# A graph layer on one core: the attention's linear part as columns of the projection's weights, a Gram block moved among the projected chunks, the takes planned anew, the RMS weights loaded as rows

## The reference

```python
xn = layernorm(x)
# attention over the graph (GATv2)
h = (xn * rsqrt(mean(xn**2) + 1e-6) * rms_w) @ W_down          # 1024 -> 256
xl, xr = h @ Wl, h @ Wr                                        # 4 heads of 64
msg = xl[src] + xr[dst]                                        # loops added
e = einsum(where(msg > 0, msg, 0.2 * msg), att)
p = exp(e - segment_max(e, dst)); alpha = p / segment_sum(p, dst)
gnn = segment_sum(alpha * xl[src], dst) @ W_up                 # 256 -> 1024
# linear attention without softmax
q, k, v = xn @ Wq.T + bq, xn @ Wk.T + bk, xn @ Wv.T + bv
mix = ((q @ k.T) * SCALE) @ v @ Wo.T + bo
x = x + gnn + mix
# feed-forward on values rounded to FP4 blocks of 16
g, u = fp4(layernorm(x)) @ fp4(gate_w).T, fp4(layernorm(x)) @ fp4(up_w).T
x = x + fp4(silu(g) * u) @ fp4(down_w).T
```

## Time and profile before

| | us |
|---|---|
| runs: median (lowest to highest), 3 runs | 902.01 (901.41 to 905.28) |
| the profiled execution: its time | 905.27 |
| the profiled execution: span of the instructions | 903.4 |
| TensorE busy | 855.8 (95%) |
| VectorE busy | 794.7 (88%) |
| ScalarE busy | 563.1 (62%) |
| GpSimd busy | 497.2 (55%) |

### The profile page before, as it was taken

How to read it: one execution, slowest core, us unless ns; L and a number is a source line. 1 busy time by engine, 2 the same in 40 slices (tenths; PEclk the granted TensorE clock), 3 DMA queues, 4 the chain that set the end, 5 groups by cost and what they waited for, 6 DMA issues and landing times.

```text
span 903.4 us, 9499 instructions
## 1 busy us (share of the span) xinstructions
PE 855.8 (95%) x2744; PEld 421.2 (47%) x2754; DVE 794.7 (88%) x903; ACT 563.1 (62%) x1977; POOL 497.2 (55%) x527
## 2 busy tenths in 40 slices
PE   6899999999999999999999999999699999999855
PEld 5786455644444444444444444444244444444322
DVE  6999989689999999999999999999993078788994
ACT  3317532387658778779898988789894243243432
POOL 3405588667667677777777878877751130010001
PEclk7989999999999999999999999999699999999878
DMA  9331773735354433554336634338936563222335
GB/s 300 112 124 25 230 200 102 246 89 88 73 177 148 122 88 102 192 186 120 100 99 195 195 97 103 90 92 193 265 84 134 116 155 93 79 43 46 47 47 88
DMA packets 66578, 114.83 MB, mean 127 GB/s; under 512 B 29575, under 2 KB 36516, under 8 KB 66506
## 3 DMA queue, kind: packets, MB, share of 16 engines
q0 software_dynamic: 22144, 63.68, 30.2%
q1 hardware_dynamic: 44378, 50.51, 17.4%
HBM read 89.28 MB, written 17.17 MB: 118 GB/s over the span
## 4 chain that ended last, share of the span: by engine, by line
DVE 59%; PE 32%; issue 4%; ACT 3%; DMA 1%; SPq 0%; ACTq 0%; POOL 0%; DVEq 0%
PE acc L782 21%; DVE acc_sb L1540 11%; DVE z L1703 10%; DVE turned L1532 10%; DVE turned L1701 10%; PE acc L939 2%; PE acc L972 2%; PE turned L939 2%; PE acc L942 2%; PE turned L996 1%; ACT round_mem L1177 1%; DVE z L1708 1%; DVE big_b L1492 1%; DMA big_b<-in_x 1%; DVE big_a L1495 1%
## 5 line engine op out<-in xcount | busy, mean ns | idle before, releaser
L564 POOL DMA_INDIRECT round_mem<-msg_table,idx x352 | 349.5, 993 | 103.0 <-issue 82.6
L1177 ACT ACTIVATE round_mem<-round_mem,pz 128x65 f32<-128x65 f32 x1408 | 354.0, 398 | 6.8 <-DVE acc_sb L1540 2.8
L782 PE MATMUL acc<-wslot,big_a 128*128 128x512 f32 x512 | 220.3, 593 | 0.0
L782 PEld LDWEIGHTS acc<-wslot,big_a 128*128 128x128 f32 x512 | 97.3, 190 | 121.3 <-issue 121.1
L1540 DVE TENSOR_REDUCE acc_sb<-round_mem 128x260 f32<-128x1820 f32 (+1 forms) x62 | 121.6, 1962 | 14.1 <-ACT round_mem L1177 12.0
L782 PE MATMUL acc<-big_b,wslot 128*128 128x512 f32 x256 | 110.0, 593 | 0.0
L782 PE MATMUL acc<-wslot,big_b 128*128 128x512 f32 x256 | 110.0, 593 | 0.0
L1532 DVE TENSOR_TENSOR turned<-round_mem,turned 128x1560 f32<-128x1560 f32 (+1 forms) x62 | 105.4, 1700 | 2.3 <-DMA round_mem<-msg_table,idx 0.2
L1703 DVE TENSOR_REDUCE z<-turned 128x24 f32<-128x1560 f32 (+1 forms) x62 | 105.1, 1696 | 2.1
L1167 ACT ACTIVATE pz<-z 128x7 f32<-128x7 f32 (+1 forms) x248 | 55.4, 295 | 78.9 <-DVE z L1708 77.9
L1701 DVE SCALAR_TENSOR_TENSOR turned<-turned,att_sb 128x1536 f32<-128x1536 f32 (+1 forms) x62 | 103.6, 1671 | 0.1
(11 more groups left out here) (231 smaller groups left out, 1009.8 us busy)
## 6 DMA issues: line engine op xcount, KB each, us to landing
big_b<-in_x SPq DMA_DIRECT2D x12, 512.0 KB, 9.8
round_mem<-msg_table,idx POOLq DMA_INDIRECT x352, 2.8
big_b<-big_b POOLq DMA_DIRECT2D x9, 512.0 KB, 5.9
out_x<-big_b SPq DMA_DIRECT2D x9, 512.0 KB, 3.1
out_x<-acc_sb POOLq DMA_DIRECT2D x9, 512.0 KB, 5.6
wslot<-in_wv_t SPq DMA_DIRECT2D x2, 2048.0 KB, 9.9
wslot<-in_wk_t SPq DMA_DIRECT2D x2, 2048.0 KB, 9.4
wslot<-in_wo_t SPq DMA_DIRECT2D x2, 2048.0 KB, 9.6
```

Source lines behind the costliest of these rows:

```text
L564: pool.indirect_dma_start(xg[g % 4][:, j, :], None, msg_table, bass.IndirectOffsetOnAxis(idx[:, c, j0 + j:j0 + j + 1], 0)).then_inc(xg_in[ ...
L782: mm = nc.tensor.matmul(o(acc[:, n % 4, :]), a, b, start=first, stop=last)
L1177: ins = nc.scalar.activation(to[:, :, j], xg[g % 4][:, j, h * HR + 1:(h + 1) * HR], ACT.Copy, scale=pz[:, g % 2, j, h:h + 1])
```

## The change

- **Linear part.** Wl and Wr are stored head by head as 65 columns (`wlr_sb`, 1 + 64), and VectorE writes -0.2 times the linear weights into the first column of each head. A chunk is two lr groups of 260 columns, one for Wl and one for Wr; the products into `lin_ps` and the 20 small takes go. ScalarE takes 260 columns in one instruction (the last chunk's Wl group in two). Wl and Wr come by four DMAs, in pieces of 256 B.
- **Gram block.** Gram block 0 stands behind the fourth lr group, the order of the first eight blocks is another, and ScalarE ranks six chunks of nodes there in one go before it takes the block.
- **Plan.** The constants of the planning loop change, ScalarE may be given a bank that is full up to 2.5 later than the round's begin, and its banks count as free 3.6 after it. The sums for the bias start a round earlier.
- **RMS weights.** They come as 8 rows of 128, are transposed by TensorE and copied by ScalarE to `rms_col`.
- **Tail.** SiLU waits for the gate half of the product (`gate_full`), VectorE for the whole (`gu_full`); the last chunk's gate and up product stands ahead of the down product of its turn.

```diff
-PRODUCTS_AT, GROUP_STEP = 168, {"p0c": 2.0, "bias": 1.0}
-ROUND_0_AT, SLOT_STEP, ROUND_OVER, TAKE_STEP = 158, 0.95, 2.2, 0.7
+PRODUCTS_AT, GROUP_STEP = 169.5, {"p0c": 2.0, "bias": 1.0}
+ROUND_0_AT, SLOT_STEP, ROUND_OVER, TAKE_STEP = 166.5, 0.95, 2.2, 0.7
...
-BIAS_SUMS_AT, AHEAD = 43, 2
+BIAS_SUMS_AT, AHEAD = 42, 2
...
-GRAM = [(m, 1) for m in (4, 0, 5, 1, 6, 2, 7, 3)] + [(m, 0) for m in (0, 4, 1, 5, 2, 6, 3, 7)]
+GRAM = [(m, 1) for m in (0, 4, 1, 5, 2, 6, 3, 7)] + [(m, 0) for m in (0, 4, 1, 5, 2, 6, 3, 7)]
...
-    g += [("lr", c, "act") for c in range(C)]
-    for kind, eng in (("gram", "act"), ("p", "dve"), ("kv", "dve"), ("t1", "act"), ("t2", "act")):
+    g += [("lr", i, "act") for i in range(4)] + [("gram", 0, "act")] + [("lr", i, "act") for i in range(4, 2 * C)]
+    g += [("gram", i, "act") for i in range(1, 16)]
+    for kind, eng in ( ("p", "dve"), ("kv", "dve"), ("t1", "act"), ("t2", "act")):
...
-        wlr_sb = big_a[:, KB * HID:KB * HID + 4 * HID].rearrange("p (k d) -> p k d", k=2)
-        hid_t = big_a[:, 3072:3072 + 2 * NP].rearrange("p (k n) -> p k n", k=2)
+        wlr_sb = big_a[:, KB * HID:KB * HID + 4 * H * MR].rearrange("p (b h d) -> p b h d", b=4, h=H)
...
-                    with nc.allow_non_contiguous_dma(reason="columns of small vectors"):
-                        sp.dma_start(rms_col[:], rms_w.rearrange("(k p) -> p k", p=P)).then_inc(rms_in, 16)
+                    sp.dma_start(rms_rows[:], rms_w.rearrange("(k p) -> k p", p=P)).then_inc(rms_in, 16)
...
-            sp.dma_start(wlr_sb[:, :, 0:HID], wl.rearrange("(k p) d -> p k d", p=P)).then_inc(wlr_in, 16)
-            sp.dma_start(wlr_sb[:, :, HID:2 * HID], wr.rearrange("(k p) d -> p k d", p=P)).then_inc(wlr_in, 16)
+            for k in range(2):
+                for side, w in enumerate((wl, wr)):
+                    sp.dma_start(wlr_sb[:, 2 * k + side, :, 1:MR],
+                                 w[k * P:(k + 1) * P, :].rearrange("p (h d) -> p h d", h=H)).then_inc(wlr_in, 16)
...
-            sp.wait_ge(lin_taken, 1)
+            sp.wait_ge(lr_taken, 1)
+            sp.wait_ge(acc_taken["act"], taken[index_of["lr", 2 * C - 1]])
...
-            for c in range(2):
-                turn_rows(c)
+            turn_rows(0)
+            pe.wait_ge(rms_in, 16)
+            nc.tensor.transpose(rms_ps, rms_rows[:], ident[0:KB, 0:KB]).then_inc(rms_tp, 1)
+            turn_rows(1)
...
-            for c in range(C):
-                pe.wait_ge(acc_taken["act"], taken[index_of["hid", 2 * (c // 2) + 1]])
-                group("lr", c, [(lambda a: a[0:NC, :], hid_t[:, k, c * NC:(c + 1) * NC], wlr_sb[:, k, :],
-                                 k == 0, k == 1) for k in range(2)])
-                for k in range(2):
-                    mm = nc.tensor.matmul(lin_ps[:, c, :], hid_t[:, k, c * NC:(c + 1) * NC],
-                                          watt[:, 2 * k:2 * k + 2, :].rearrange("p a h -> p (a h)"), start=(k == 0), stop=(k == 1))
-            mm.then_inc(lin_full, 1)
...
+            for i in range(2 * C):
+                c, side = divmod(i, 2)
+                if i == 4:
+                    gram(0)
+                if side == 0:
+                    pe.wait_ge(acc_taken["act"], taken[index_of["hid", 2 * (c // 2) + 1]])
+                group("lr", i, [(lambda a: a[0:NC, 0:H * MR], hid_t[:, k, c * NC:(c + 1) * NC],
+                                 wlr_sb[:, 2 * k + side, :, :].rearrange("p h d -> p (h d)"), k == 0, k == 1) for k in range(2)])
...
-                mm.then_inc(gu_full, 1)
+                    mm.then_inc(gate_full if h == 0 else gu_full, 1)
...
+                if k + 1 == C - 1:
+                    gate_up(k + 1)
                 if 0 <= k - 2 < C:
                     down(k - 2)
-                if 0 <= k + 1 < C:
+                if 0 <= k + 1 < C - 1:
...
-                full = max(at, freed.get(n - 4, 0)) + GROUP_STEP.get(kind, 7.0)
-                if full > begun:
+                full = max(at, freed.get(n - 4, 0)) + GROUP_STEP.get(kind, 6.93)
+                if full > begun + (2.5 if engine == "act" else 0.0):
                     break
                 round_of[n], at = g, full
                 begun += TAKE_STEP if engine == "dve" else 0.0
-                freed[n] = begun + 0.8
+                freed[n] = begun + (0.8 if engine == "dve" else 3.6)
...
+                    both = a[0:NC, 0:H * MR].rearrange("p (h d) -> p h d", d=MR)
+                    to = (acc_sb, xr_sb)[side][:, c, :].rearrange("p (h d) -> p h d", h=H)
+                    scale = rrms[:, c:c + 1]
+                    if side == 0 and c == C - 1:
+                        nc.scalar.activation(to[:, :, 0], both[:, :, 0], ACT.Identity, scale=scale, bias=far_col[:, 0:1]).then_inc(lr_taken, 1)
+                        nc.scalar.activation(to[:, :, 1:MR], both[:, :, 1:MR], ACT.Copy, scale=scale).then_inc(t, 1)
+                    else:
+                        nc.scalar.activation(to[:, :, 0:MR], both, ACT.Copy, scale=scale).then_inc(t, 1)
...
-            act.wait_ge(rms_in, 16)
+            act.wait_ge(rms_tp, 1)
+            nc.scalar.copy(rms_col[:], rms_ps).then_inc(rms_taken, 1)
+            act.wait_ge(rms_taken, 1)
             act.wait_ge(wd_in, 16)
-            for k in range(3):
+            for k in range(2):
...
-            for c in range(3):
-                rank(c)
+            rank(0)
             for c in range(C):
-                take(index_of["lr", c])
-                if c + 3 < C:
-                    rank(c + 3)
-            act.wait_ge(lin_full, 1)
-            for c in range(C):
-                nc.scalar.activation(acc_sb[:, c, 0:ROW:HR], lin_ps[:, c, 0:H], ACT.Identity, scale=rrms[:, c:c + 1],
-                                     bias=far_col[:, 0:1] if c == C - 1 else 0.0)
-                ins = nc.scalar.activation(xr_sb[:, c, 0:H * MR:MR], lin_ps[:, c, H:2 * H], ACT.Copy, scale=rrms[:, c:c + 1])
-            ins.then_inc(lin_taken, 1)
...
-                    act.wait_ge(gu_full, c + 1)
+                    act.wait_ge(gate_full, c + 1)
...
-                                         wlr_sb.rearrange("p k (a h d) -> p (k a) h d", a=2, h=H),
+                                         wlr_sb[:, :, :, 1:MR],
...
-            nc.vector.tensor_scalar(watt[:], watt[:], -SLOPE, None, ALU.mult).then_inc(watt_done, 1)
+            nc.vector.tensor_scalar(wlr_sb[:, :, :, 0], watt[:], -SLOPE, None, ALU.mult).then_inc(watt_done, 1)
...
+                    dve.wait_ge(gu_full, c + 1)
```

More of the change, by code:

```diff
@@ L853, in sum_places @@
                     pe.wait_ge(sort_part, 2)
[L855 removed]
+            for i in range(1, 16):
                 if i == 8:
                     sum_places()
[L858 to L866 removed]
+                gram(i)
             def halves_in(kind, i, first_use):
@@ L1130, in _ @@
             act.wait_ge(key_in, 32)
[L1131 to L1132 removed]
+            rank(0)
             for c in range(C):
[L1134 to L1142 removed]
+                take(index_of["lr", 2 * c])
+                take(index_of["lr", 2 * c + 1])
+                if c == 1:
+                    for i in range(1, 7):
+                        rank(i)
+                    take(index_of["gram", 0])
+                if 7 <= c + 5 < C:
+                    rank(c + 5)
             for i in range(16):
[L1144 removed]
+                if i > 0:
+                    take(index_of["gram", i])
                 if i < KB:
```

42 lines of the change are left out of this document (20 added, 22 removed).

## The result

The changed kernel takes 881.96 us (median of 4 runs, 881.28 to 882.76), the kernel before 903.49 (4 runs, 901.41 to 905.28): a ratio of 0.976, 95% interval 0.974 to 0.979. That is 21.5 us less; forecast were 23.3, and 879. The profiled execution took 882.22 us, span 880.5.

The account below looks back on a forecast made before the run. TensorE and VectorE were both taken as bounds in the long middle. RMS rows 3.8, projection 3.7, replanned takes 12.5 and tail 3.3 sum to 23.3 us off the 902.0 median: 879 forecast, range 870 to 892.

Parts of the forecast that it names:

- The RMS rows: Start of the kernel: loading the RMS weights as rows starts VectorE's third chunk sooner and saves 3.8 us.
- Without rms_col W_down begins ... near 5.3: First loads: without the column load ahead of it, W_down starts near 5.3 us instead of 9.7, 4 us sooner.
- The lower bound of 1.0: Start of the kernel: the RMS weights' gain is only 1.0 us if VectorE's gain does not pass on.
- The projection and the Gram block: Linear part before the attention: four products of 260 columns a chunk and the new order save 3.7 us, bounds 2.5 and 4.4.
- The replanned takes: Long middle: 72 takes moved one to three rounds earlier close TensorE's two waits, saving 12.5 us, bounds 6 and 13.4.
- kv 10: Product n = 27 in the rounds: VectorE's worst wait for a full bank, 3.2 us.
- too tight: Rival, rounds: early takes make them later than 3.3 us and the attention ends last; 886 at 10 us late; chance 0.16.
- Such waits don't add: Rounds: once late, all later slacks are larger, so rounds are late by 3.2 us at most, 2 to 2.5 at the end.
- The slower rival: Rounds: each of 41 earlier ScalarE takes costs beyond the cover; a loss from 27.5 us late on, 0.67 a take; chance 0.03.
- The tail: After the attention: SiLU waiting for the gate half only and the last gate product's order save 3.3 us, bounds 1 and 5.
- one lies off the path: Tail: of VectorE's three waits for ScalarE's normalization, 4.2 us in all, one does not count, leaving 2.0 us.
- sum of the upper bounds: Whole kernel: all four parts at their upper bounds save 26.7 us, giving 875.3 us.

## Why the prediction was right, and where it was not

The sum of 23.3 us came out as 21, with the mechanisms as forecast in three of four parts. In the fourth, the load of the RMS weights, the mechanism was not there. That the time still came within 3 us of 879 is in part luck: 3.8 us were missing there, and the runs found up to 1.8 more in the tail than the sum had.

**The RMS rows: 3.8 forecast, 0.1 measured.** The step that failed is "Without rms_col W_down begins ... near 5.3". It took the order of landings in one trace for a cause: rms_col landed late in it, W_down later, the chunk last. In two other traces with the column the chunk starts at 11.7, as with the rows. Late landings of rms_col and of W_down came together (7.4 and 9.9 us, against 4.7 and 5.0 with 8.2), and which of them makes the other late, or whether both have one cause, no run shows. The slow microsecond is real (76 GB/s in the stretch 5 to 6 of both, 61 in the earlier trace rows, 150 with the rows), but 74 GB/s more for 1 us are 0.07 MB, which is 0.2 us at 418 GB/s, and even that isn't seen. The rule of the Trainium skill (DMA: Bandwidth & Descriptors, "Why a DMA increments its semaphore by 16 and not by 1") says when a DMA counts as landed. I drew from it what a late landing does to the next DMA, which it doesn't say, and the runs don't bear it out: behind the column W_down landed 8.2 us after its issue in two of three traces, behind the rows 7.6 to 8.6 in nine. The lower bound of 1.0 was too high as well. That the projection started at 12.43 instead of 14.52 belongs in the main to the same chance: with the column back it started at 12.38, and in the second trace of before at 13.29. The four loads of Wl and Wr in small pieces, priced at up to 6 us if uncovered, were covered: no engine waits for their landing in the changed kernel's two traces.

**The projection and the Gram block: 3.7 forecast, 3.2 measured** (21.55 - 18.34 in the traces; no run undoes this part whole). A chunk takes 1.755 us, 1.75 were forecast. A small matmul of before thus cost (2.16 - 1.755)/4, some 0.10 us. The Trainium skill (TensorE: Matmul & The Clock Gate, "Back-to-back issue gap") was weighed here with its 25 ns, which it gives as a floor and not as a price; the same section says that in a stream each matmul's weight load counts too. The trace of before agrees: each of the four had a weight load of 128x128, and three of these follow each other in 0.41 us, some 0.11 apart, where one is busy 0.19:

```profile
79.24 0.41 PEld L836 LDWEIGHTS turned<-watt,big_a 128*128 128x128 f32 x3 [0.24 <-issue]
```

TensorE waited some 0.8 us where 1.0 was forecast. That both halves must go together was not in the prediction: the columns alone lose 2.2 us, since ScalarE's 2.31 us a chunk, which I had as the price of a rank and two takes, then is the step.

**The replanned takes: 12.5 forecast, 12.3 measured,** 13.46 between the first traces. The worst wait was forecast at kv 10 with 3.2 us; VectorE stood 1.0 us there and 3.0 in four waits. The rounds end 2.0 us late, 2 to 2.5 were forecast. The forecast that the attention then lands just before TensorE needs it holds. My formula for the case "too tight" (697.5, less what the products start sooner, plus what the rounds are late) can be held to the run with earlier takes: 697.5 - (175.40 - 170.28) + (527.5 - 511.5) = 708.4, and TensorE started its transposes at 708.29 (511.5 is 686.92, the last close of the trace before, less 175.40). What does not hold is "Such waits don't add". Held against the run with takes a round later, where VectorE never waits for a product (510.6 us), the changed kernel's rounds are late by 2.9 us with waits of 3.0, and those of the run with earlier takes by 16.9 with waits of 14.3. In these three runs the waits add in full, and more. What is limited is their number: once the rounds were late enough, after 304 us, there were no more. And I missed how they can feed themselves, by TensorE waiting for sums that VectorE, late itself, makes late. The slower rival, late by 27.5 us, was not reached even there.

**The tail: 3.3 forecast, 5.1 measured by the runs, 3.4 between the first traces.** SiLU gave 4.1 (2.0 forecast), in the traces 3.1. The mis-sized step is "one lies off the path": none did, and a wait of VectorE for SiLU itself, 0.73 us, was not counted; 2.4 and 0.73 are the 3.1. The order (1.3 forecast) gave 1.0 in the runs and nothing in the traces; that it is worth anything isn't shown. The tail, from the attention's first transposes to the end, differs by itself: 183.0 to 186.6 us in the nine traces that have the changed one, 189.2, 189.2 and 190.9 in the three that have the old one. So 5.1 carries an uncertainty of more than a microsecond, and a wait of up to 0.9 us for the additions, which TensorE meets now that it is at the tail's start sooner, is in it.

Together: 0.1 + 3.2 + 12.3 + 5.1 = 20.7; measured 903.2 - 882.5 = 20.7, with the middle of all runs of both kernels. Three of the four terms are differences of medians that may each be off by about 1 us, so that the sum fits so closely is partly luck too.

The prediction's sum of the upper bounds is wrong: 4.9 + 4.4 + 13.4 + 5 are 27.7 and not 26.7, which makes 874.3 us and not 875.3. Nothing else hangs on it.

Of the signs named ahead, these came: the second Gram block (97.4, forecast 96), the start of the products (169.4, forecast 168), no idle time of TensorE before the transposes, these at 694.7 (forecast 693 to 695), the waits of VectorE (0.2 to 1.2 us each, 3.0 in all), and the last down product, 24.0 us sooner (896.19 and 872.17, forecast 23). One did not: the third chunk at 11.6 and not 9.6.

## What to carry to other kernels

A wait of the first microseconds, read from one trace, is to be seen in a second execution of the same kernel before it is priced: here near half of the first difference up to the first product was chance. When a step on one engine is shortened, look at once at the engine that empties its banks; its step can become the bound, and here reordering its other work let the gain through. A plan of hand-overs is best set a little late where several buffers hold the producer: 5 us to the late side cost nothing here, 5 us to the early side 14.

## What the runs showed of the hardware that I had not expected

Two profiled executions of one kernel, apart by nothing else, started the first product at 169.37 and 171.11, most of it by how long TensorE stayed at 1.2 GHz behind a stand of 2.40 and 2.69 us at 40 us (16 matmuls in 4.32 and 5.77 us, 3.62 at 2.4 GHz). The same 4 KB load of single floats landed 4.7, 5.0 and 7.4 us after its issue in three executions, one of the changed kernel with the column and two of the kernel before. And a stand of 4.04 us in the middle of full work cost TensorE nearly as much again: its clock was granted at 0.83 in the stretch 270 to 290, which is 3.4 us, and the products behind it were 3.6 late beyond the stand. In the changed kernel, which doesn't stand there, the same stretch has 1.00. A float32 matmul of 8 columns took as long as the distance of its 128x128 weight loads, some 0.1 us.
